# Attention: the exponents' products of the second and sixth place move behind the value products of a step

## The reference, cut to what matters

```python
x = L0_attn_x                                   # (8, 512, 256)
x = x + attn(layernorm(x), Wq, bq, Wk, bk, Wv, bv, Wo, bo)
x = x + ffn(layernorm(x), ...)                  # 16 experts, 512 tokens each, and a shared one

def attn(x, ...):                               # 16 heads of 16, window 64, key and query 0 global
    Q, K, V = split_heads(x @ Wq + bq), split_heads(x @ Wk + bk), split_heads(x @ Wv + bv)
    scores = einsum('bhqd,bhkd->bhqk', Q, K) * scale + longformer_mask(512)
    out = einsum('bhqk,bhkd->bhqd', softmax(scores), V)
    return merge_heads(out) @ Wo + bo
```

## Time and profile before

| what | us |
|---|---|
| median of 3 runs | 1311.2 |
| lowest, highest | 1307.7, 1317.17 |
| the profiled execution | 1312.74 |
| its span, first to last instruction | 1311.0 |
| PE busy in the span | 1176.8 (90%) |
| DVE, ACT, POOL busy | 866.9, 607.0, 608.6 |
| first score matmul, last value product's copy | 117.8, 451.3 |

### The profile page before, as it was taken

The page is one execution under the profiler, slowest core; times in us unless marked ns, Lnnn a source line. Parts: engine busy times, 40 slices in busy tenths (PEclk is TensorE's granted clock), DMA queues, the critical chain, the costliest instruction groups (busy, mean ns, idle before and its releaser), DMA issues. The chain is left out here.

```text
span 1311.0 us, 23503 instructions
## 1 busy us (share of the span) xinstructions
PE 1176.8 (90%) x8906; PEld 969.1 (74%) x8906; DVE 866.9 (66%) x2246; ACT 607.0 (46%) x959; POOL 608.6 (46%) x698
## 2 busy tenths in 40 slices
PE   0997799999999627999997799999999999999997
PEld 0885566666666426988886588888888888888886
DVE  7895577777777146856887766667676667666641
ACT  1340466666666524443221554445555555454442
POOL 8000244444444544522000467666666666665654
PEclk9997799999999967899998799999999999999999
DMA  2589476677675276410031443443444344444311
GB/s 90 196 284 148 118 119 107 111 122 113 112 113 88 69 218 180 126 53 17 33 125 42 155 120 97 122 128 121 129 124 122 101 127 102 124 128 105 105 33 17
DMA packets 62350, 149.09 MB, mean 114 GB/s; under 512 B 14992, under 2 KB 31776, under 8 KB 52896
## 3 DMA queue, kind: packets, MB, share of 16 engines
q1 hardware_dynamic: 49584, 128.72, 38.2%
q0 software_dynamic: 12656, 18.90, 8.1%
HBM read 104.73 MB, written 42.34 MB: 112 GB/s over the span
## 5 line engine op out<-in xcount | busy, mean ns | idle before, releaser
L553 DVE CUSTOM_DVE_ANT_0 junk_s<-ps_s,mask 128x258 bf16<-128x258 f32 (+2 forms) x512 | 210.1, 471 | 91.3 <-PE ps_s L629 91.0
L1779 POOL TENSOR_TENSOR h_lo<-h,h_hi 128x512 fp32r<-128x512 f32 x128 | 177.3, 1398 | 129.5 <-ACT h_hi L1815 129.2
L606 ACT ACTIVATE pt<-ps_p 128x516 f32<-128x516 f32 (+2 forms) x256 | 173.1, 680 | 109.6 <-PE ps_p L650 78.9
L477 POOL TENSOR_SCALAR_AFFINE_SELECT pt<-pt 128x256 f32<-128x256 f32 x352 | 132.2, 415 | 187.1 <-ACT pt L606 187.1
L1889 PE MATMUL ps_gu<-xt_hi,w_hi 128*128 128x512 f32 x512 | 203.8, 398 | 2.1 <-DVE xt_lo L1838 2.1
L1889 PE MATMUL ps_gu<-xt_lo,w_hi 128*128 128x512 f32 x512 | 201.1, 393 | 0.0
L1889 PE MATMUL ps_gu<-xt_hi,w_lo 128*128 128x512 f32 x512 | 200.6, 392 | 0.0
L1854 DVE TENSOR_TENSOR h<-ge,ps_gu 128x512 f32<-128x512 f32 x128 | 87.9, 686 | 169.5 <-ACT ge L1809 156.1
L1716 DVE TENSOR_TENSOR w_lo<-w,w_hi 128x768 fp32r<-128x768 f32 x128 | 173.8, 1362 | 31.3 <-ACT w_hi L1711 27.8
L629 PE MATMUL ps_s<-ks,qs 96*128 96x258 f32 (+2 forms) x512 | 166.9, 372 | 17.6 <-PEq L191 9.0
L1788 POOL DMA_INDIRECT out<-ys,idx x64 | 127.3, 1989 | 72.3 <-ACT ys L1825 57.4
(11 more groups left out here) (220 smaller groups left out, 2412.2 us busy)
## 6 DMA issues: line engine op xcount, KB each, us to landing
w<-in_We SPq DMA_DIRECT2D x48, 1024.0 KB, 4.9
qk_parts<-qk SPq DMA_DIRECT2D x8, 2064.0 KB, 7.8
qs<-qk_parts SPq DMA_DIRECT2D x96, 129.0 KB, 3.9
ks<-qk_parts SPq DMA_DIRECT2D x96, 129.0 KB, 5.6
x<-in_x SPq DMA_DIRECT2D x16, 512.0 KB, 8.1
attn_t<-on SPq DMA_DIRECT2D x32, 256.0 KB, 5.7
ot<-attn_t SPq DMA_DIRECT2D x16, 256.0 KB, 4.5
rd<-rden SPq DMA_DIRECT2D x16, 256.0 KB, 4.1
```

The source lines that it names most:

```text
L477: last = pool.affine_select(out=part, in_=part, pattern=[[0, HQ], [sign, WIN]], compare_op=ALU.is_ge, fill=0.0, base=sign * (n % 2) * WIN, ...
L553: dve.tensor_tensor_reduce(junk[:, (u * SG + g) % RING, 0:n], ps_s[:, (u * SG + g) % RING, 0:n], m, 1.0, -3e38, ALU.add, ALU.max, mx[:, u ...
L606: act.activation(dst, src, ACT.Exp, scale=SCALE).then_inc(exp_s, 1)
L1779: pool.tensor_tensor(h_lo[:, m], h32[:, (e * KI + m) % HB], h_hi[:, m].bitcast(F32), ALU.subtract).then_inc(hlo_s, 1)
```

## The change

In PE's order the scores and the value products are regrouped: behind the exponents of place 0 (and 4) come the scores of place 1 (and 5), then the value products, and only then the exponents of place 1 (and 5). On ACT `out_rows` of the step before moves from behind exp 7 to behind exp 6.

```diff
                         act.activation(dst, src, ACT.Exp, scale=SCALE).then_inc(exp_s, 1)
-                        if n == 7 and u >= 1:
+                        if n == 6 and u >= 1:
                             out_rows(u - 1)
...
+                def scores(u, n):
+
+                    if u < NU:
+                        score(u, 2 * n)
+                        score(u, 2 * n + 1)
...
                     for n in range(SJ):
-                        if u + 2 < NU:
-                            score(u + 2, 2 * n)
-                            score(u + 2, 2 * n + 1)
+                        if n not in (1, 5):
+                            scores(u + 2, n)
                         exponents(u, n)
-                        if u >= 1 and n in (1, 5):
-                            times_v(u - 1, n // 2)
-                            times_v(u - 1, n // 2 + 1)
+                        if n in (0, 4):
+                            scores(u + 2, n + 1)
+                            if u >= 1:
+                                times_v(u - 1, n // 2)
+                                times_v(u - 1, n // 2 + 1)
```

## The result

| | before | after |
|---|---|---|
| median | 1310.18 us (20 runs) | 1319.45 us (20 runs) |
| lowest, highest | 1304.91, 1320.15 | 1312.79, 1325.74 |
| span of the profiled execution | 1311.0 | 1315.5 |
| first score to the start of the last copy out of `ps_o`, in the trace | 333.5 | 343.0 |
| a step (median of 28 steps) | 9.67 | 9.91 |

The ratio is 1.0072, 95% interval 1.0054 to 1.0089: the change costs 9.3 us. The attention alone became 9.5 us longer, 6.5 up to the last score and 3.0 behind it. (Every fourth step is 0.4 us longer in both kernels: it holds DVE's reciprocal of 0.51 us, L569.) The stages behind the attention took 859.7 us before and 855.4 after in these two executions. They are the same code in all kernels of this study and scattered between 852 and 864 us, whichever attention stood in front.

What follows compares the result with a forecast made beforehand. PE and DVE were taken to bound the step in turn. 29 x (-0.08 + 0.25) = +4.9 us and +1.1 at the end gave +6.0, a median of 1317 us, range 1309 to 1324.

Steps and rivals of the forecast that it cites:

- What bounds the step: Attention step: PE and DVE bound it in turn, two stretches each; DVE's idle 1.50 us at the first value products stays.
- PE's stretch S1b to S2a: PE from the last score before the first value products to the next score: 0.08 us shorter a step.
- PE's stretch S5b to S6a: PE from the last score before the second value products to the next score: change 0, with 0.11 us either way.
- The wait for exp 1: PE's exponents of place 3 wait 0.37 us for ACT's exponential of place 1; DVE runs dry for 0.25 us a step.
- E3: PE's exponent pair of place 3 in a step: its load waits 0.37 us for ACT's exponential of place 1.
- GpSimd's masks start later by the same time, and their product is used a step later: GpSimd's mask work in a step: it shifts with the exponential of place 5, later by 1.03 us.
- ACT's other waits: Waits on ACT's exponentials of places 2, 5, 6 and 7 in a step: they hold.
- rival B: ACT becomes the bound of the step's second stretch too: step 0.6 us longer, 1330 us; chance 0.08.
- The end, +1.1: Last two steps, without scores: the second exponential waits for the value products, +1.1 us, between 0 and +2.4.
- Sum: Whole kernel: 29 x (-0.08 + 0.25) = +4.9 and +1.1 at the end, +6.0 us; 1317 us, chance 0.63.
- rival A: No net change: DVE's slack absorbs the wait at place 3's exponents, or they are not late; 1310 us; chance 0.25.
- C: Rival: waits before both value product blocks and changes of tile disappear; needs 0.45 us a step, 1298.5 us; chance 0.04.

Runs made afterwards that it cites:

- short_exp1: The changed kernel with ACT's second exponential of a step cut from 1024 to 384 columns from step 2 on; step 9.68 us.
- few_zero: The changed kernel with only the last of each block's 3 or 4 zeroings by POOL, the others left out; step 9.80 us.

## Why the prediction was right or wrong, point by point

**What bounds the step**: right. PE and DVE bound it in turn, and S1b and S5b are the places where the one hands over to the other. The regrouping moved no score as against the value products, and DVE's idle time at V01 went from 1.50 to 1.38 us only.

**PE's stretch S1b to S2a, -0.08 us**: right. 0.10 by short_exp1, and DVE's first maximum behind V01 starts 3.17 us after S1b's load (310.17 to 313.34) where it was 3.28 (307.46 to 310.74).

**PE's stretch S5b to S6a, 0**: right in effect. Measured between the starts of the products it grew from 1.59 to 1.69, with S6a to S6b shrinking from 0.20 to 0.09: S6a's weights are now loaded behind E5, as its working said of S2a.

**The wait for exp 1**: right in mechanism and place, a little large in size. E3 waits 0.28 us where 0.37 was worked out, DVE runs dry and S5b comes 0.23 us later where 0.25 was taken. With the gain of PE the stretch grew by 0.13 for 0.17, which is 1.2 us in 29 steps. The release was taken rightly: exp 1 ends at 313.22 + 1.02 = 314.24 and E3's load follows 0.05 us behind (314.29). That E3 waits 0.28, as an earlier release would have given, has another reason: counted from S1b's load, exp 1 came 0.05 us sooner than worked out (3.05 for 3.10) and E3 was ready 0.04 later (314.01).

**"GpSimd's masks start later by the same time, and their product is used a step later"**: this is the step that failed. The product was indeed not late, no value product waits for it. But the work itself moved onto DVE's tail and held up L559 by 0.115 us in every step, on the one stretch that DVE bounds. The forecast asked only who waits for POOL, not what runs beside it. 29 x 0.115 is 3.3 us, a cost for which the sum has no term.

**ACT's other waits** (rival B): they held; S5b to S1b grew by no more than the collision explains, as few_zero shows.

**The end, +1.1**: 1.6 by the order, inside its bounds of 0 to 2.4. In the profiled execution another 1.4 came from the granted clock, for which the forecast had no term.

**Sum**: 29 x 0.24 = 7.0 (the traces have 6.5 up to the last score) and 1.6 or 3.0 at the end, 8.1 to 10.0, against 6.0 forecast and 9.3 measured. The time, 1319.45, lies in the range of 1309 to 1324, but in part by luck: the 3.3 us that no term held were met by 1.2 us too much in another and by a range that was wide for other reasons, for rival A and for the end. Of the rivals none came true: A fell with the wait at E3, which short_exp1 alone removes; B and C by the step times, 0.24 us longer where B needed 0.6 longer and C 0.45 shorter.

## What to carry to other kernels

An instruction moved behind a long block delays what depends on it through every engine: here PE's E5, ACT's exp 5 and then POOL's zeroing, whose only cost was that it met one small DVE instruction of the tail. Ask of each piece of work that shifts not only who waits for it, but also what it will run beside. And where two engines bound a loop in turn, the queue between them should be full as the long block begins and be fed first as it ends; filler work belongs in front of an instruction that would wait anyway, which was worth 0.44 us a step here against the 0.1 that swapping sides could have given at best.

## What was not expected of the hardware

A DVE instruction on 128 x 16 elements takes 0.175 us alone. Where it starts beside one of POOL's `affine_select` of 0.415 us, it ends 0.01 to 0.03 us behind that one, so it takes between 0.22 and 0.39 us by the moment at which it starts, and 0.175 if it starts 0.29 to 0.32 us into it. Of the 309 held up in the 14 traces, two, which started 0.36 us into one, ended behind the next. That holds for the one with two inputs in SBUF (L559) and for one with one input (L557); the transposition and the maxima of 258 columns with one input in PSUM keep their times. And the clock can fall within the last microseconds of a stage: from 1.00 to 0.51 behind 8.5 us in which PE was busy for 6.70, where it ended at 1.00 in the kernel before behind 8.4 us with 6.56.
